# Joining the first stages of a two-layer block into one program section, and loading the expert layers' weights one stage ahead

## The chip, the cores and the metric

The kernel runs on one core of one Trainium2 chip. Its time is the device time of one execution in microseconds (us). The core has a matrix engine (TensorE, in the profile PE, its weight loads PEld), a vector engine (VectorE, DVE), an activation engine (ScalarE, ACT), a general engine (GpSimd, POOL) and a control engine (SyncE, SP) that in this kernel issues nearly all transfers (DMAs). The engines run side by side and wait for each other by semaphores. The work is written as a row of blocks; a block begins when all five engines have left the one before.

## The reference

Two layers are applied to x (64 sequences of 32 tokens, 512 wide). Cut to what matters:

```python
def _L0_cond_ref(u, length, log_dt, C, log_A_real, A_imag, D):
    mask = (jnp.arange(Lq) < length[:, None]).astype(u.dtype)
    u_m = u * mask[:, None, :]
    kernel = _get_kernel(log_dt, C, log_A_real, A_imag, Lq)      # filter taps, 32 filters of 512
    y = irfft(rfft(u_m) * rfft(kernel))[..., :Lq]                # a causal convolution
    return (y + u_m * D[:, None]) * mask[:, None, :]
def _L0_ffn_ref(x, W_base, b_base, W_gate, A, B):                # _L1_ffn_ref has the same form
    result = x @ W_base.T + b_base
    probs = softmax(x @ W_gate.T)                                # 8 experts, the two best are used
    h = einsum('bnd,erd->bner', x, A)
    return result + einsum('bner,eor->bno', h * route_w, B) * SCALING
x = x + _L0_ffn_ref(_L0_cond_ref(x, ...), ...)
x = x + _L1_ffn_ref(_L1_cond_ref(x, ...), ...)                   # paged attention with rotary positions
```

`_get_kernel` sums 64 damped complex exponentials for each filter. The attention layer reads a cache of keys of 64 pages, and turns query and key by angles that depend on the position.

## The kernel before, in words

The blocks run in this order.

1. `s4d_taps`. SP loads the constants, the filter parameters, the lengths, x in reversed order (`um`, 4 tiles of 1 MB) and the first key pages. DVE computes the filter taps in one long chain of small and middle-sized instructions, in which ACT computes sines; POOL masks `um` by the lengths. PE turns (transposes) the cache of keys in 16 pieces (`turn_keys`): 8 pieces, then the 64 small products that make the taps, then the other 8. ACT copies each turned piece out of PSUM, SP stores it and loads the next piece. When all 16 are stored, SP writes the taps to DRAM.
2. `convolve`. For each of 32 filters SP reads the taps back in Toeplitz form (`cv_toe`, 256 KB), PE multiplies, DVE masks the result into `y_t`. POOL computes the rotary angles from the positions, which SP loads after the first 8 Toeplitz tiles (`cv_leni`, read in single elements); ACT computes their sines.
3. `ffn`, first time (tag 0). SP loads the layer's weights (`f_g`, `f_bias`, `f_a`, `f_w`, `f_lb`). PE computes the gate's logits (L585), turns them (L590), and DVE picks the two best experts in a chain of 19 instructions (L516 to L539). For each of four column groups PE computes `h` (L613), the base product (L620, 16 matrix products in 32 records of the profile), turns the routing weights (L598), spreads them (L604), and adds the expert product (L627). POOL computes the rotary tables `ta` and `tb` meanwhile.
4. `project`, `attention`, `output_projection`, which the diff touches only by one call.
5. `ffn`, second time (tag 1), and the end.

In `ffn` the semaphore `s_ev` counts results taken out of the PSUM banks 1 to 4. Before the base product of each bank PE waits for `s_ev`, and DVE gives the first four counts as credits only after the routing chain is done:

```python
                done["route"] = line.n
                credits(e, s_ev, KB)
```

In `s4d_taps` the step size `log_dt` is read straight into the layout in which it is used, in single elements of 4 bytes:

```python
                    src = bass.AP(tensor=dram["L0_cond_log_dt"].tensor, offset=half, ap=[[0, NS], [2, HP]])
```

The order of the work is written out by hand. An engine does its instructions in that order, and a wait holds up all that stands behind it on its engine.

Of the kernel before, what the change touches and what calls it, by code (L numbers as in the profile page):

```python
# [15 lines left out]
F32 = mybir.dt.float32  # L16
# [128 lines left out]
def s4d_taps(nc, ps, dram, taps, cst, um, mrow, k_t):  # L145
# [6 lines left out]

    with ExitStack() as ctx:
        sb = lambda n, s, d=F32: ctx.enter_context(nc.sbuf_tensor("s4_" + n, s, d))
        sem = lambda n: ctx.enter_context(nc.semaphore("s4_" + n))
        TB = 4
        k_in = sb("k_in", [P, TB, HK * D])
        k_out = sb("k_out", [P, TB, PPT, HK, PSIZE])
        s_kt, s_kc = sem("kt"), sem("kc")
        s_ki, s_ko = ([sem(f"{n}{q}") for q in range(TB)] for n in ("ki", "ko"))  # L160
        leni = sb("leni", [P, B], I32)
        lenf = sb("lenf", [P, B])
        mrev = sb("mrev", [P, KB, B])
# [6 lines left out]
        shape = [P, HP, NMUL]  # L170
        arg, mag, t1, t2, t3, ang, sa, ca, sn, cs, er, ei = (
            sb(n, shape) for n in ("arg", "mag", "t1", "t2", "t3", "ang", "sa", "ca", "sn", "cs", "er", "ei"))
# [3 lines left out]
        s_in, s_v, s_sin, s_u, s_k, s_ev, s_out, s_len, s_x, s_g = (  # L176
            sem(n) for n in ("in", "v", "sin", "u", "k", "ev", "out", "len", "x", "g"))
        done = {}
        mul = cst[:, C_MUL:C_MUL + NMUL]
        with nc.Block() as block:  # L180
            @block.sync
            def _(e):
                e.dma_start(cst[:, :], dram["cst"]).then_inc(s_in, 16)
                for half in range(2):
                    src = bass.AP(tensor=dram["L0_cond_log_dt"].tensor, offset=half, ap=[[0, NS], [2, HP]])
                    e.dma_start(raw[half * NS:(half + 1) * NS, 0, :], src, allow_slow_non_contiguous=True).then_inc(s_in, 16)
# [4 lines left out]
                src = bass.AP(tensor=dram["itok_B_8_3872"].tensor, offset=0, ap=[[0, P], [1, B]])  # L191
                e.dma_start(leni[:, :], src).then_inc(s_len, 16)
                for k in range(KB):
                    e.dma_start(um[:, k, :, :], dram["x_rev"][k * P:(k + 1) * P, :, :]).then_inc(s_x, 16)

                for n in range(TB):
                    e.dma_start(k_in[:, n, :], dram["k_cache"][n * P:(n + 1) * P, :]).then_inc(s_ki[n], 16)
                k_rows = k_t.rearrange("(t n d) x -> t d n x", n=PPT, d=P)

                def store(t, q):  # L200
                    e.wait_ge(s_kc, (t + 1) * 2 + 2)
                    t = slice(t, t + 1) if isinstance(t, int) else bass.ds(t, 1)
                    e.dma_start(k_rows[t, :, :, :].rearrange("o d n x -> (o d) n x"),
                                k_out[:, q, :, :, :].rearrange("p n g k -> p n (g k)")).then_inc(s_ko[q], 16)

                with e.Fori(0, KT // TB - 1) as i:
                    for q in range(TB):
                        store(i * TB + q, q)
                        e.dma_start(k_in[:, q, :], dram["k_cache"][bass.ds((i * TB + q + TB) * P, P), :]).then_inc(s_ki[q], 16)
                for q in range(TB):  # L210
                    store(KT - TB + q, q)
                for q in range(TB):
                    e.wait_ge(s_ko[q], 16 * KT // TB)

                e.wait_ge(s_ev, 1)
                e.dma_start(taps[:, P:KPW].rearrange("h (a b) -> a h b", b=32),
                            kev[:, :, :, :].rearrange("a i t b -> a (i t) b")).then_inc(s_out, 16)
                e.dma_start(taps[:, 0:P], zeros[:, :]).then_inc(s_out, 16)
                e.wait_ge(s_out, 32)

            @block.vector
            def _(e):
# [3 lines left out]
                e.wait_ge(s_in, 16 * 7)  # L226
                flat = lambda x: x.rearrange("p a b -> p (a b)")
# [8 lines left out]
                mulb = spread(mul, 1, HP)  # L236
                v(lambda e: e.tensor_tensor(ang[:, :, :], spread(dai, 2, NMUL), mulb, ALU.mult))
                reduce_angle(v, flat(ang[:, :, :]), flat(t1[:, :, :]), flat(sa[:, :, :]), flat(ca[:, :, :]))
                done["angles"] = line.n
                v(lambda e: e.tensor_tensor(arg[:, :, :], spread(dar, 2, NMUL), mulb, ALU.mult))  # L240
                exp_exact(v, flat(arg[:, :, :]), flat(mag[:, :, :]), flat(t1[:, :, :]), flat(t2[:, :, :]), flat(t3[:, :, :]))
# [4 lines left out]
                zr, zi, nr, ni, t, u = w[3], ei[:, :, 1], w[4], w[5], w[6], w[7]  # L246
# [3 lines left out]
                v(lambda e: e.tensor_tensor(t, ci, zi, ALU.mult))  # L250
                v(lambda e: e.tensor_tensor(nr, nr, t, ALU.subtract))
                v(lambda e: e.tensor_tensor(ni, cr, zi, ALU.mult))
                v(lambda e: e.tensor_tensor(t, ci, zr, ALU.mult))
                v(lambda e: e.tensor_tensor(ni, ni, t, ALU.add))
                sr, si, den = w[8], w[9], w[10]
                v(lambda e: e.tensor_tensor(sr, nr, ar, ALU.mult))
                v(lambda e: e.tensor_tensor(t, ni, ai[:, :], ALU.mult))
                v(lambda e: e.tensor_tensor(sr, sr, t, ALU.add))
                v(lambda e: e.tensor_tensor(si, ni, ar, ALU.mult))
                v(lambda e: e.tensor_tensor(t, nr, ai[:, :], ALU.mult))  # L260
                v(lambda e: e.tensor_tensor(si, si, t, ALU.subtract))
                v(lambda e: e.tensor_tensor(den, ar, ar, ALU.mult))
                v(lambda e: e.tensor_tensor(t, ai[:, :], ai[:, :], ALU.mult))
# [1143 lines left out]
```

## Time and profile before

| | |
|---|---|
| time, median of 3 runs | 2720.36 us (2719.50 to 2720.91) |
| the profiled execution's own time | 2722.63 us |
| its span | 2720.6 us |
| busy, share of the span | PE 93%, PEld 79%, DVE 69%, ACT 47%, POOL 30% |
| DMA, mean over the span | 187 GB/s |
| first block begins, second block's first transfer | 0 us, 109.18 us |
| first `ffn`: first product of the gate | 173.55 us |
| second `ffn`: first product of the gate | 2597.58 us |

The time of a run and the span of its trace differ by 2 us, which lie before and after the span. The busy shares are means over stages with quite different limits: over most of the span PE is busy nine tenths of each slice, in the first slices it is not.

### The profile page before, as it was taken

The numbers are of one execution on the slowest core, as the hardware profiler recorded it, in microseconds if no ns is written. First come the engines' busy times: TensorE is split into PE (matmuls) and PEld (weight loads), VectorE is DVE, ScalarE is ACT, GpSimd is POOL, SyncE is SP. The second block draws the span as 40 slices with busy tenths as digits, with TensorE's granted clock in tenths as the row PEclk, the third lists the DMA queues.
The fourth block names the chain that finished last, engine by engine and source line by source line (L and its number), as shares of the span: only waits on it lengthen the run. The fifth ranks groups of instructions, "written<-read, shape, count | busy, mean of one in ns | idle before, by whom it ended". The sixth has DMA issues, their size and how long they took to land. (4 is left out here: it accounts for less than half of the span.)

```text
span 2720.6 us, 53012 instructions
## 1 busy us (share of the span) xinstructions
PE 2540.0 (93%) x15632; PEld 2139.9 (79%) x15632; DVE 1867.8 (69%) x3327; ACT 1282.3 (47%) x3654; POOL 808.8 (30%) x743
## 2 busy tenths in 40 slices
PE   2479899999998899999999999999999979999989
PEld 1453588777776689999999999999999967777733
DVE  5242599999995088888888888888888854444311
ACT  1101355555553256666666666666666641111100
POOL 3070166666663022222222222222222231212000
PEclk9689999999998999999999999999999989999989
DMA  5441133332334478888888888888888844343212
GB/s 193 162 158 62 58 96 109 94 95 93 112 93 138 146 251 272 295 271 290 276 290 273 291 274 292 274 286 279 288 277 286 280 149 124 108 123 108 62 69 79
DMA packets 432385, 508.52 MB, mean 187 GB/s; under 512 B 39860, under 2 KB 352468, under 8 KB 431828
## 3 DMA queue, kind: packets, MB, share of 16 engines
q1 hardware_dynamic: 395476, 373.71, 41.9%
q0 software_dynamic: 36864, 134.23, 15.5%
q8 instruction: 25, 0.41, 0.1%
q14 instruction: 20, 0.16, 0.0%
HBM read 407.07 MB, written 100.75 MB: 187 GB/s over the span
## 5 line engine op out<-in xcount | busy, mean ns | idle before, releaser
L1079 PE MATMUL ps<-at_v_raw,at_pt 128*128 128x128 f32 x4096 | 541.1, 275 | 0.6 <-DMA at_v_raw<-v_cache,at_idx 0.6
L1079 PEld LDWEIGHTS ps<-at_v_raw,at_pt 128*128 128x128 f32 x4096 | 497.7, 192 | 1.0 <-DMA at_v_raw<-v_cache,at_idx 1.0
L1179 ACT ACTIVATE at_pt<-ps 128x512 f32<-128x512 f32 x512 | 305.1, 596 | 339.8 <-PE ps L1063 326.1
L1146 DVE CUSTOM_DVE_ANT_0 at_sm<-ps,at_mask 128x544 f32<-128x544 f32 x512 | 367.9, 719 | 91.3 <-PE ps L1054 45.4
L868 POOL TENSOR_TENSOR pr_m<-pr_qn,tb 128x256 f32<-128x256 f32 x320 | 331.6, 1056 | 311.7 <-DVE pr_qn L837 296.5
L1190 ACT ACTIVATE at_pr<-at_sm,at_nm 128x544 f32<-128x544 f32 x512 | 383.9, 750 | 72.1 <-DVE at_nm L1146 59.5
L1017 POOL DMA_INDIRECT at_v_raw<-v_cache,at_idx x256 | 307.5, 1201 | 113.1 <-issue 62.3
L702 PE MATMUL ps<-pr_hi,xh 128*128 (+1 forms) x768 | 319.8, 416 | 13.1 <-DVE pr_lo L691 8.7
L1139 DVE TENSOR_TENSOR at_k_lo<-shared,at_k_hi 128x1088 fp32r<-128x1088 f32 x256 | 325.5, 1272 | 0.0
L1054 PE MATMUL ps<-at_k_hi,at_q_hi 128*128 128x272 f32 x1024 | 295.9, 370 | 13.5 <-DVE at_k_lo L1139 13.5
L1063 PE MATMUL ps<-constants,at_pr 128*128 128x128 f32 x2048 | 307.9, 273 | 0.0
L703 PE MATMUL ps<-pr_lo,xh 128*128 (+1 forms) x768 | 305.4, 398 | 0.0
L704 PE MATMUL ps<-pr_hi,xl 128*128 (+1 forms) x768 | 304.5, 397 | 0.0
L795 ACT ACTIVATE pr_sq<-ps 128x128 f32<-128x128 f32 x640 | 168.0, 277 | 235.6 <-DVE pr_ss L830 225.1
L1023 POOL COPY at_idx<-at_rows 128x4 uint32 (+1 forms) x64 | 12.1, 189 | 799.5 <-PE ps L1086 795.6
L1063 PEld LDWEIGHTS ps<-constants,at_pr 128*128 128x128 f32 x2048 | 245.0, 140 | 0.5 <-issue 0.5
L1292 DVE TENSOR_TENSOR att<-att,ps 128x512 f32<-128x512 f32 x128 | 79.4, 682 | 220.1 <-PE ps L1312 220.1
L1054 PEld LDWEIGHTS ps<-at_k_hi,at_q_hi 128*128 128x128 f32 x1024 | 165.8, 192 | 74.4 <-issue 72.8
L1310 PE MATMUL ps<-op_o_hi,op_w_hi 128*128 128x512 f32 x512 | 205.6, 402 | 16.4 <-POOL op_w_lo L1251 16.4
L1054 PE MATMUL ps<-at_k_hi,at_q_lo 128*128 128x272 f32 x1024 | 214.6, 291 | 0.0
L1054 PE MATMUL ps<-at_k_lo,at_q_hi 128*128 128x272 f32 x1024 | 211.5, 288 | 0.0
L1312 PE MATMUL ps<-op_o_hi,op_w_lo 128*128 128x512 f32 x512 | 205.4, 401 | 0.0
(197 smaller groups left out, 4423.1 us busy)
## 6 DMA issues: line engine op xcount, KB each, us to landing
shared<-k_t SPq DMA_DIRECT2D x1024, 128.0 KB, 4.3
qk_t<-pr_stage SPq DMA_DIRECT2D x160, 256.0 KB, 2.3
shared<-qk_t SPq DMA_DIRECT2D x64, 512.0 KB, 7.7
o_t<-at_ot SPq DMA_DIRECT2D x64, 512.0 KB, 5.9
o_raw<-o_t SPq DMA_DIRECT2D x32, 1024.0 KB, 5.9
w_first<-wqkv SPq DMA_DIRECT2D x12, 1024.0 KB, 5.9
s_k_in<-k_cache SPq DMA_DIRECT2D x16, 512.0 KB, 7.2
k_t<-s_k_out SPq DMA_DIRECT2D x16, 512.0 KB, 6.3
```

The lines of the kernel that those rows point to most:

```text
L702: e.matmul(out, xh[:, k, cols], hi, start=(k == 0), stop=False)
L703: e.matmul(out, xh[:, k, cols], lo, start=False, stop=False)
L704: last = e.matmul(out, xl[:, k, cols], hi, start=False, stop=(k == KB - 1))
L868: ins = e.tensor_tensor(heads(m2[:, q, :])[:, :, a], heads(qn[:, q, :])[:, :, b], table(tb, i, j - 3, a), ALU.mult)
L1017: e.indirect_dma_start(out=v_raw[:, q, c, :], out_offset=None, in_=dram["v_cache"], in_offset=bass.IndirectOffsetOnAxis(ap=idx[:, q, c:c + ...
L1054: last = e.matmul(ps[:, 2 * r + h, 0:W], a[:, q, mine], b[:, w, g % 2, h * W:(h + 1) * W], start=first, stop=end)
L1063: last = e.transpose(ps_w[:, c * P:(c + 1) * P], pr[:, w, k, c * P:(c + 1) * P], ident)
L1079: last = e.matmul(ps[:, 5 + w, k * D:(k + 1) * D], pt[:, r, c * P:(c + 1) * P], v_raw[:, q, c, g * D:(g + 1) * D], start=(k == 0 and c == ...
L1139: e.tensor_tensor(two(k_lo), raw, two(k_hi).bitcast(F32), ALU.subtract).then_inc(s_lo, 1)
L1146: e.tensor_tensor_reduce(out=halves(sm[:, r, :]), in0=ps[:, 2 * r:2 * r + 2, 0:W], in1=halves(mask[:, q, :]), scale=-SC, scalar=3e38, op0= ...
L1179: e.activation(pt[:, r, :], ps_w, ACT.Copy).then_inc(s_pt, 1)
L1190: e.activation(pr[:, w, k, :], sm[:, r, :], ACT.Exp, bias=nm[:, at], scale=-1.0, accum_out=su[:, at]).then_inc(s_e, 1)
```

## The change

The two first blocks become one, `prologue`. In it:

- `log_dt` is read as whole rows to all partitions and picked apart by two DVE copies; so is the list of positions, which DVE picks apart with four copies.
- The constants, the lengths, the positions, `um` and the zeros of the taps are loaded or stored by ACT's queue, beside SP's.
- `um` is no longer masked. The output row was masked before and still is.
- PE turns 9 pieces of keys, makes the taps, and then runs the convolution, with one of the other 7 pieces behind every fourth filter. ACT copies the taps out of PSUM, writes them, and issues the Toeplitz loads, between its copies of the late pieces. There are 6 Toeplitz buffers in place of 8.
- The rotary angles are computed by DVE, between the taps and the first convolution result, in 10 instructions (POOL before, in 13).

In `ffn` the weights are loaded by the block before: at the end of `prologue`'s list on SP, and behind the first group of the output projection. The credits are gone: the base products of the first column group wait for nothing. POOL begins the rotary tables only when the routing chain is done. Some buffers share one room of memory, and `w_first` moves to the other side of it.

```diff
-def s4d_taps(nc, ps, dram, taps, cst, um, mrow, k_t):
+def prologue(nc, ps, dram, taps, cst, um, mrow, k_t, y_t, cos, sin, room, inputs):
...
-                e.dma_start(cst[:, :], dram["cst"]).then_inc(s_in, 16)
-                for half in range(2):
-                    src = bass.AP(tensor=dram["L0_cond_log_dt"].tensor, offset=half, ap=[[0, NS], [2, HP]])
-                    e.dma_start(raw[half * NS:(half + 1) * NS, 0, :], src, allow_slow_non_contiguous=True).then_inc(s_in, 16)
+                src = bass.AP(tensor=dram["L0_cond_log_dt"].tensor, offset=0, ap=[[0, P], [1, S]])
+                e.dma_start(log_dt[:, :], src).then_inc(s_in, 16)
...
+                for n in range(KT):
+                    e.wait_ge(s_kc, 2 * (n + 1))
+                    e.dma_start(k_rows[n:n + 1, :, :, :].rearrange("o d n x -> (o d) n x"),
+                                k_out[:, n % TB, :, :, :].rearrange("p n g k -> p n (g k)")).then_inc(s_ko[n % TB], 16)
+                    if n + TB < KT:
+                        load(n + TB)
+                inputs.load(e, dram, ("w0", "b0", "g0", "a0", "lb0"))
...
-                e.wait_ge(s_x, 16 * KB)
-                for k in range(KB):
-                    e.tensor_tensor(um[:, k, :, :], um[:, k, :, :], spread(mrev[:, k, :], 1, S), ALU.mult)
...
             @block.scalar
+                e.dma_start(cst[:, :], dram["cst"]).then_inc(s_cst, 16)
+                for n, name in enumerate(("itok_B_8_3872", "itok_B_207_1644")):
+                    src = bass.AP(tensor=dram[name].tensor, offset=0, ap=[[0, P], [1, B]])
+                    e.dma_start(leni[:, n, :], src).then_inc(s_len, 16)
+                for k in range(KB):
+                    e.dma_start(um[:, k, :, :], dram["x_rev"][k * P:(k + 1) * P, :, :]).then_inc(s_x, 16)
...
+                e.wait_ge(s_ev, 1)
+                e.dma_start(taps[:, P:KPW].rearrange("h (a b) -> a h b", b=32),
+                            kev[:, :, :, :].rearrange("a i t b -> a (i t) b")).then_inc(s_out, 16)
+                e.wait_ge(s_out, 32)
+                for h in range(TOE):
+                    load(h)
+                e.wait_ge(s_v, done["rope"])
+                for x in (sin, cos):
+                    e.activation(x, x, ACT.Sin).then_inc(s_rope, 1)
+                for h in range(S):
+                    if h + TOE < S:
+                        e.wait_ge(s_mm, h + 1)
+                        load(h + TOE)
+                    if late(h):
+                        lay_out(late(h))
...
             @block.tensor
+                for h in range(S):
+                    e.wait_ge(s_toe[h % TOE], 16 * (h // TOE + 1))
+                    wait(e, s_y, h - YB + 1)
+                    for d in range(KB):
+                        last = e.matmul(ps[:, h % YB, d * B:KB * B], toe[:, h % TOE, d * P:(d + 1) * P],
+                                        um[:, 0:KB - d, h:h + 1, :].rearrange("p k o b -> p k (o b)"),
+                                        start=(d == 0), stop=(d == KB - 1))
+                    last.then_inc(s_mm, 1)
+                    if late(h):
+                        turn(late(h))
@@ ffn @@
-                credits(e, s_ev, KB)
...
+                    e.wait_ge(s_nw, 32)
+                    e.wait_ge(s_v, done["route"])
+                    rope_tables(e, s_tab, tables[0], tables[1], nw, tables[2], tables[3])
...
-                        e.wait_ge(s_ev, i * KB + ob + 1)
+                        wait(e, s_ev, (i - 1) * KB + ob + 1)
@@ output_projection @@
                 turn(0)
+                inputs.load(e, dram, ("w1", "b1", "g1", "a1", "lb1"))
```

On SP the transfers of the first block stood in this order before (`s_raw` takes `log_dt` and `log_a`, `s_ai`, `s_cc` and `s_dvec` the other filter parameters):

```order
L183 DMA constants<-cst 128x897
L186 DMA s_raw<-L_cond_log_dt 64x16x1 x2
L187 DMA s_raw<-log_a 128x16
L188 DMA s_ai<-a_imag 128x16
L189 DMA s_cc<-c 128x32
L190 DMA s_dvec<-L_cond_D 1x32
L192 DMA s_leni<-itok_B_3872 128x64
L194 DMA um<-x_rev 128x2048 x4
L197 DMA s_k_in<-k_cache 128x1024 x4
```

Now the same place on SP reads:

```order
L191 DMA s_log_dt<-L_cond_log_dt 128x32
L192 DMA s_raw<-log_a 128x16
L193 DMA s_ai<-a_imag 128x16
L194 DMA s_cc<-c 128x32
L195 DMA s_dvec<-L_cond_D 1x32
L198 DMA s_k_in<-k_cache 128x1024 x4
```

The constants, the lengths and `um` have left SP's list. They stand on ACT, whose list from the start of the block to the first convolution's refills is:

```order
L301 DMA constants<-cst 128x897
L304 DMA s_leni<-itok_B_3872 128x64
L304 DMA s_leni<-itok_B_1644 128x64
L306 DMA um<-x_rev 128x2048 x4
L308 DMA taps<-s_zeros 32x128 [waits s4_v]
...
L333 ACTIVATE s_kev<-ps 16x16x32 [waits s4_k]
...
L336 DMA taps<-s_kev 16x32x32 [waits s4_ev]
L322 DMA s_toe<-taps 128x512 [waits s4_out]
...
L343 ACTIVATE shared<-shared 128x1024 [waits s4_v]
...
L322 DMA s_toe<-taps 128x512 [waits s4_mm] x4
L316 ACTIVATE s_k_out<-ps 128x4x4x32 [waits s4_kt,s4_ko1]
L316 ACTIVATE s_k_out<-ps 128x4x4x32 [waits s4_kt]
```

Each Toeplitz refill now waits on ACT for PE (`s4_mm`), and four refills stand between two copies of a turned piece (`s4_kt`). On PE the first column group of `ffn` read before:

```order
L613 MATMUL ps<-shared,f_a 128x512 [waits f0_in]
L613 MATMUL ps<-shared,f_a 128x512 x3
L620 MATMUL ps<-shared,f_w 128x512 [waits f0_ev]
L620 MATMUL ps<-shared,f_w 128x512 x3
...
L598 MATMUL ps<-constants,f_route 8x128 [waits f0_v]
```

and reads now:

```order
L592 MATMUL ps<-shared,f_a 128x512 [waits f0_s_in]
L592 MATMUL ps<-shared,f_a 128x512 x3
L599 MATMUL ps<-shared,f_w 128x512 x16
L577 MATMUL ps<-constants,f_route 8x128 [waits f0_v]
```

The four waits for `f0_ev` are gone from the 16 base products; the wait for the routing chain (`f0_v`) stands behind them, at the turning of the routing weights.

## Rows read from the trace of the kernel before

**Rows 1.** Stretches: busy PE, PEld, DVE, ACT, POOL, then PE clock, DMA share, GB/s.

```profile
5.00:10.00 5.00, 0.00 (x0) 0.00 (x0) 0.00 (x0) 0.00 (x0) 0.00 (x0) 1.00 0.05 0
30.00:35.00 5.00, 0.00 (x0) 0.00 (x0) 4.69 (x10) 0.00 (x0) 2.47 (x4) 1.00 1.00 418
77.00:84.00 7.00, 6.44 (x125) 6.44 (x126) 0.47 (x2) 0.00 (x0) 0.00 (x0) 0.50 0.01 2
142.00:150.00 8.00, 8.00 (x54) 7.64 (x54) 4.02 (x7) 0.00 (x0) 7.75 (x4) 0.99 0.70 189
```

**Rows 2.** Instructions in order of time: start, us, engine, line, operation, count.

```profile
1.19 1.45 SPq L186 DMA_DIRECT2D s_raw<-L_cond_log_dt  x2
```

**Rows 3.** The same view, the chain of the taps on DVE with POOL beside it.

```profile
27.11 0.18 DVE L114 TENSOR_SCALAR s_raw<-s_raw 128x32 f32<-128x32 f32 x1 [26.13 <-DMA s_dvec<-L_cond_D]
31.11 0.96 DVE L237 TENSOR_TENSOR s_ang<-s_small,constants 128x768 f32<-128x768 f32 x1
36.87 0.56 DVE L140 TENSOR_SCALAR s_ang<-s_sa 128x768 f32<-128x768 f32 x1
36.97 19.99 POOL L296 TENSOR_TENSOR um<-um,s_mrev 128x2048 f32<-128x2048 f32 x4 [4.21 <-DMA um<-x_rev]
37.46 4.75 DVE L141 TENSOR_SCALAR s_ca<-s_sa 128x768 f32<-128x768 f32 x1
42.24 5.13 DVE L142 TENSOR_TENSOR s_ca<-s_ang,s_ca 128x768 f32<-128x768 f32 x1
47.41 5.18 DVE L240 TENSOR_TENSOR s_arg<-s_small,constants 128x768 f32<-128x768 f32 x1
52.62 4.75 DVE L114 TENSOR_SCALAR s_arg<-s_arg 128x768 f32<-128x768 f32 x1
77.56 0.28 PE L336 MATMUL ps<-s_er,s_ur 64*16 64x32 f32 x2 [11.88 <-DVE s_ui L276]
```

**Rows 4.** The same view, from the taps' products to the end of the convolution.

```profile
84.28 5.31 PE L326 MATMUL ps<-constants,s_k_in 128*128 128x128 f32 x32
92.61 1.09 PE L326 MATMUL ps<-constants,s_k_in 128*128 128x128 f32 x8 [3.02 <-DMA s_k_in<-k_cache]
109.18 3.71 SPq L364 DMA_DIRECT2D cv_toe<-taps  x8
112.64 12.55 PE L396 MATMUL ps<-um,cv_toe 128*128 x64 [10.21 <-DMA cv_toe<-taps]
137.32 31.43 PE L396 MATMUL ps<-um,cv_toe 128*128 x192 [12.12 <-DMA cv_toe<-taps]
```

**Rows 5.** Transfers by line: count, KB each, median us from issue to landing.

```profile
cv_toe<-taps SPq DMA_DIRECT2D x32, 256.0 KB, 3.5
cv_leni<-itok_B SPq DMA_DIRECT2D x4, 2.0 KB, 15.2
taps<-s_kev SPq DMA_DIRECT2D x1, 64.0 KB, 2.4
```

**Rows 6.** The same view, the first `ffn` and what precedes the second.

```profile
173.55 15.24 PE L585 MATMUL ps<-shared,f_g 128*8 128x512 f32 x32 [4.80 <-DMA f_g<-g]
190.55 3.70 PE L613 MATMUL ps<-shared,f_a 128*128 128x512 f32 x8
207.58 15.39 PE L620 MATMUL ps<-shared,f_w 128*128 128x512 f32 x32 [13.33 <-DVEq L101]
2592.20 2.48 DVE L1292 TENSOR_TENSOR att<-att,ps 128x512 f32<-128x512 f32 x4 [8.88 <-PE ps L1312]
```

**Rows 7.** Who waited for whom, PE, from 2560 us to the end.

```profile
PE ps L585 <- DMA f_g<-g: 5.4, 1, 5.4
PE ps L620 <- DVEq L101: 2.6, 1, 2.6
```

**Rows 8.** The chain of waits that ended last, its end: start, us, step.

```profile
2622.29 15.70 PE ps L620 x32
2653.20 13.93 PE ps L620 x32
```

More of the change, by code:

```diff
@@ L196, in _ @@
                 for n in range(TB):
-                    e.dma_start(k_in[:, n, :], dram["k_cache"][n * P:(n + 1) * P, :]).then_inc(s_ki[n], 16)
+                    load(n)
                 k_rows = k_t.rearrange("(t n d) x -> t d n x", n=PPT, d=P)
[L200 to L204, printed above, removed]
@@ L225, in _ @@
                 v(lambda e: e.memset(zeros[:, :], 0.0))
-                e.wait_ge(s_in, 16 * 7)
-                flat = lambda x: x.rearrange("p a b -> p (a b)")
+                done["zeros"] = line.n
+                e.wait_ge(s_in, 16 * 5)
+                for half in range(2):
+                    part = slice(half * NS, (half + 1) * NS)
+                    mine = log_dt[part, :].rearrange("p (i two) -> p two i", two=2)[:, half:half + 1, :].rearrange("p o i -> p (o i)")
+                    v(lambda e, part=part, mine=mine: e.tensor_copy(raw[part, 0, :], mine))
                 w = [small[:, i, :] for i in range(12)]
@@ new lines, in _ @@
+                v(lambda e: e.tensor_scalar(pos[:, :], pos[:, :], cst[:, C_MOD:C_MOD + 1], None, ALU.add))
+                e.wait_ge(s_kv, 2)
+                d = kev[0:1, :, :, 0:1].rearrange("a i t b -> a (i t b)")
+                e.tensor_tensor(d, d, dvec[:, :], ALU.add).then_inc(s_ev, 1)
+                v(lambda e: e.tensor_tensor(f, spread(pos[:, :], 2, H), spread(cst[:, C_FREQ:C_FREQ + H], 1, NT), ALU.mult))
+                reduce_angle(v, flat(f), flat(t), flat(sin), flat(cos))
+                done["rope"] = line.n
@@ L330, in _, with turn @@
-                turn_keys(0, 2)
+                def turn(n):
+                    q = n % TB
+                    e.wait_ge(s_ki[q], 16 * (n // TB + 1))
+                    wait(e, s_kc, 2 * (n - 1))
+                    for half in range(2):
+                        for g in range(HK // 2):
+                            x = slice((half * HK // 2 + g) * D, (half * HK // 2 + g + 1) * D)
+                            last = e.transpose(ps[:, 4 + 2 * (n % 2) + half, g * P:(g + 1) * P], k_in[:, q, x],
+                                               cst[:, C_ID:C_ID + P])
+                        last.then_inc(s_kt, 1)
@@ L331, in _ @@
+                e.wait_ge(s_cst, 16)
+                for n in range(EARLY):
+                    turn(n)
                 e.wait_ge(s_u, 1)
@@ L434, in rope_tables, with __init__, load, ffn @@
     e.tensor_scalar(tb[:, :, 0:H], tb[:, :, 0:H], -1.0, None, ALU.mult)
[L437 to L443 removed]
+class Inputs:
+    def __init__(self, nc, ctx, tag, side=None):
+        sb = lambda n, s: ctx.enter_context(nc.sbuf_tensor(f"f{tag}_{n}", s, F32, side=side))
+        self.w = sb("w", [P, KB, L])
+        self.a = sb("a", [P, KB, E * R])
+        self.g = sb("g", [P, KB, E])
+        self.lb = sb("lb", [E * R, L])
+        self.bias = sb("bias", [P, KB])
+        self.s_g, self.s_in = (ctx.enter_context(nc.semaphore(f"f{tag}_{n}")) for n in ("s_g", "s_in"))
+    def load(self, e, dram, names):
+        w_n, b_n, g_n, a_n, lb_n = names
+        e.dma_start(self.g[:, :, :], dram[g_n].rearrange("(k p) e -> p k e", p=P)).then_inc(self.s_g, 16)
+        e.dma_start(self.bias[:, :], dram[b_n]).then_inc(self.s_in, 16)
+        e.dma_start(self.a[:, :, :], dram[a_n].rearrange("(k p) r -> p k r", p=P)).then_inc(self.s_in, 16)
+        e.dma_start(self.w[:, :, :], dram[w_n].rearrange("(k p) o -> p k o", p=P)).then_inc(self.s_in, 16)
+        e.dma_start(self.lb[:, :], dram[lb_n]).then_inc(self.s_in, 16)
+def ffn(nc, ps, dram, inputs, tag, act, src, out, scaling, cst, halves=None, tables=None, ahead=None):
     NB = T // 512
```

289 lines of the change are left out of this document (102 added, 187 removed).

## The prediction

> **What bounds the kernel now.** I read the slices of the span first: PE is busy nine tenths or more in most of them, so only a stage in which PE waits can give much. Two kinds are touched: everything before the first `ffn`, and the routing chains of both `ffn`s. The stretches of the start show the first cause [rows 1]: from 5 to 10 us nothing moves at all, while from 30 to 35 us the same 16 engines carry 418 GB/s. The issues before that silence [rows 2] are the two transfers of `log_dt`, 2048 elements of 4 bytes; the first DVE instruction waits until 27.11 us for the last small input queued behind them [rows 3]. Then DVE's chain sets the pace to 77.56 us, and four of its instructions take about 5 us each while POOL masks `um`; the same kinds take 0.96 and 0.56 us alone [rows 3]. The taps are made by 84.28 us, but the first Toeplitz load is issued at 109.18 us [rows 4]: eight key pieces, their stores and the end of the block lie between. The convolution itself, 112.64 to 168.75 us, stands still for 12.12 us on a Toeplitz tile [rows 4], queued behind the positions, again single elements (15.2 us to landing for 2 KB [rows 5]). In the first `ffn` the gate starts 4.80 us after the convolution for want of its weights, and the base product waits 13.33 us for the routing chain [rows 6]; in the second the two waits are 5.4 and 2.6 us [rows 7]. All of these lie on the path that sets the end, since each block waits for the one before. I go by the gate's first product, 173.55 us now [rows 6].
>
> **Step 1, inputs.** The five small loads go first on SP without the single elements. An issue takes 3.71 / 8 = 0.46 us [rows 4], 0.7 for a scattered one [rows 2], so all are out at about 3.5 us; to landing the nearest small transfer takes 2.4 us [rows 5], which is 5.9. I take 7.0, since 4 MB of `um` and the constants now flow beside them on another queue. Bounds 5.4 and 12. Saved: 27.11 − 7.0 = 20.1 us. Two copies of the new layout cost at most 0.2 us each: −0.4.
>
> The Trainium skill, page "DMA: Bandwidth & Descriptors", section "Queues, rings and completion order", says that SP's and ACT's queues are rings on the same 16 engines, which take them in turn by whole packets. By that rule a small input issued late waits for whole packets of `um`; it is rival A. No row here has two such queues at once.
>
> **Step 2, the chain on DVE.** Without the mask on POOL the four long instructions return to their twins: (4.75 − 0.56) + (5.13 − 0.96) + (5.18 − 0.96) + (4.75 − 0.56) = 16.8 us [rows 3]. POOL has nothing to do in the new block, so I take all of it. The chain was 77.56 − 27.11 = 50.45 us and becomes 50.45 − 16.8 + 0.4 = 34.1; products start at 41.1. ACT's sines now stand behind two key copies and one more table load: ready at about 22, needed at 32, so hidden. The PE products stand behind 9 turned pieces instead of 8. At 418 GB/s `um` and the first 4 pieces (6 MB) are in by about 18 us; a further piece with its store is 1 MB, 2.6 us at the same rate, so piece 9 comes at 31 to 37 us, hidden by 4 us or more; late by 4 at the worst.
>
> **Step 3, taps to Toeplitz.** The products keep their 84.28 − 77.56 = 6.7 us (clock at the lower level, 0.50 [rows 1]): done at 47.8. What followed took 109.18 − 84.28 = 24.9 us [rows 4]. Now: two small ACT copies, 1.2 us (twice 0.6, bounded by the 0.6 of a DVE result of the same order), one DVE add with its waits 0.5, issue 0.35 and landing 2.4 [rows 5]: 4.4 us. Saved 20.5. The first product follows a load by 112.64 − 109.18 = 3.5 us as before: it starts at 55.7.
>
> **Step 4, the convolution.** Eight filters took 12.55 us, the other 24 took 31.43 [rows 4], each group with a slow start after idleness. That makes (31.43 − 12.55) / 16 = 1.18 us per filter and 3.1 us per start. New: 32 × 1.18 + 3.1 = 40.9. Seven late pieces at 1.09 us each on PE [rows 4] add 7.6: 48.5, against 168.75 − 112.64 = 56.1 now. Saved 7.6. The refills: ACT issues filter h + 6 when h is done, at most 0.45 us each; two key copies (1.7 us with their gap) stand before every fourth. A refill has five filters of lead, over 6 us, for 3.5 us of landing [rows 5], so I take 0. But toes, loads and stores together are 2 MB in every 5.9 us, 340 of the 418 GB/s seen, so landing may stretch: up to +8. DVE's rotary angles (10 instructions of 0.75 to 1.3 us, scaled from 768 to 1024 columns by [rows 3], 10.5 us) start with the taps' store and end 4 us into the convolution; four PSUM banks cover 7.9 us of it: 0. The two sines behind them on ACT (about 1 us each) delay refill 7 to about 6.5 us into it; with landing 10.0, needed at 11.4: 0, at worst +2. The convolution ends at 104.2 us.
>
> **Step 5, into the first `ffn`.** The gap of 4.8 us [rows 6] becomes the last DVE result, 0.6 us, and the change of block, 1.3 us in all by my estimate: its weights are issued behind the last key store, some 3 us before the end. Saved 3.5; if that store is late, 0 to 3 less. Gate at 105.5. Sum so far: 20.1 − 0.4 + 16.8 + 20.5 + 7.6 + 3.5 = 68.1, and 173.6 − 68.1 is that 105.5.
>
> **Step 6, the first `ffn`.** The base product follows `h` at once: 13.3 us of waiting goes, and its slow start, 15.39 − 13.93 = 1.5 [rows 6, 8]. The gate took 15.24 us with a slow start of the same kind; with 1.3 us of idleness before it I take 1.0 back (0 to 1.5). The wait for the spread routing weights stays as it is, behind the base product. The routing chain gets rid of POOL beside it, but that is worth nothing on the path: slow as it was it took 3.7 + 13.3 = 17.0 us [rows 6] and now lies beside 3.7 + 13.9 = 17.6 us of products. Sum 15.8. POOL's rotary tables move to the time from routing on. There DVE takes sums out of PSUM; in the convolution DVE's results with one operand in PSUM took 4.02 / 7 = 0.57 us while POOL was busy 7.75 of 8 us [rows 1], so they are not held up. The low halves (two SBUF operands) can be, to about 2 us each in the first group; each base product gives DVE 13.9 us for little else: 0.
>
> **Step 7, the second `ffn`.** Of 5.4 us before the gate the last accumulation on DVE, 2.48 us [rows 6], and the change of block stay: 2.6 saved. The base product's wait 2.6 [rows 7] and slow start 15.70 − 13.93 = 1.8 [rows 8] go, and I add 0.5 for a shorter slow start elsewhere (0 to 3): 7.5. The five loads behind the first group of the output projection cost 5 × 0.46 us of SP and 1.5 MB (3.7 us at 418 GB/s); the tile next in line is issued about one unit of products ahead, and such a unit leaves DVE 8.88 us of idleness [rows 6], so 0, at worst 1.
>
> **Sum.** 68.1 + 15.8 + 7.5 = 91.4 us. The profiled execution would take 2722.6 − 91.4 = 2631.2 (span 2629.2, and 2.0 around it); it lies 2.3 above the median of the runs, so for the median 2720.4 − 91.4 = 2629.0. The unknown costs are one-sided, so I take 2630.
>
> **Rivals.**
> A. The small inputs wait behind `um`. `um`'s rows are 8 KB; eight rows on one engine are 64 KB, 2.5 us at 418 / 16 = 26 GB/s [rows 1]. Two of the five loads are issued after the flow of `um` begins: +5, at most +8 with the constants: 2636. For it: nothing orders the two queues. Against: the first three are out before.
> B. The refills of the convolution run dry behind ACT's key copies. +1.1 us for each of 7 pieces, or +8: 2638. For it: 340 GB/s. Against: lead of over 6 us against 3.5.
> C. The clock warms up where I left it low, since PE turns keys shortly before the taps and idles less: products half as long (−3.3), convolution start −2, expert products −2: 2622.
> D. Slower. ACT's single list turns the convolution into a round trip: if every refill came only after the filter before was done, one filter would cost 1.2 + 0.45 + 3.5 us and a share of the key copies (0.4), 5.6 us in place of 1.5. That is +129 us for 32, and 2759. It decides once a filter costs 1.5 + 91 / 32 = 4.4 us. For it: refills do wait on PE in one list with the key copies. Against: six buffers; only a missing overlap of all of them does it.
> E. The waits removed only uncover the next: PE's base product would wait as long for `f_w`, landing late. Price: most of 13.3 us, 2642. Against: it is issued before the block ends, 1 MB needs 2.5 us at 418 GB/s beside 2.4 of landing, and the gate's 15 us of products come first.
>
> **How the numbers follow.** Forecast 0.62; A 0.14; B 0.10; C 0.08; E 0.03; D 0.03. The range reaches to C and its bounds below (2614), to A and B together above (2630 + 8 + 8, and some for the block's end, 2650); outside remain D and some of C, under 2 in 10. A measurement of this kernel tells about 0.2%, 5 us, from no change; only D is slower, so faster 0.95, same 0.02, slower 0.03.
>
> **What would show it.** Right: the first DVE instruction after its inputs at 6 to 8 us; no DVE instruction of 768 columns over 1 us in the chain; taps' products at about 41; Toeplitz loads at about 52; a convolution of about 49 us with no wait over 2 us on a Toeplitz tile; the gate at 104 to 108; no wait between `h` and the base product in either `ffn`, and the wait for the expert product still there. Wrong: the gate after 115, long waits of PE on Toeplitz tiles or of DVE on its inputs, or a base product that still starts 13 us after `h`.

## Result, and the profile after

| | kernel before | kernel after |
|---|---|---|
| median of 4 runs | 2720.64 us (2719.50 to 2721.84) | 2625.51 us (2624.20 to 2627.74) |
| ratio after / before | | 0.9651, 95% interval 0.9634 to 0.9668 |
| span of the profiled execution | 2720.6 us | 2622.4 us |

The forecast was 2630.0 us, with a range of 2614 to 2650: the time lies inside it, 4.5 us below the forecast. The gain between the two profiled executions, 98.2 us of span, is 3 us larger than that of the medians, 95.1: the one before took 2722.63 us, 2.0 above its median, and the one after is the fastest of its four (2624.2 us), 1.3 below.

Two marks are read off every trace below: the first product of the first gate and of the second. With the first product of the block that follows the first `ffn` they cut the span in four.

| us of the profiled execution | before | after | gained | forecast |
|---|---|---|---|---|
| start to first gate | 173.55 | 103.36 | 70.2 | 68.1 |
| first gate to `project` | 134.0 | 116.1 | 17.9 | 15.8 |
| `project` to second gate | 2290.0 | 2286.6 | 3.4 | 2.6 |
| second gate to the end | 123.0 | 116.3 | 6.7 | 4.9 |

Stretches of the kernel after (busy PE, PEld, DVE, ACT, POOL, PE clock, DMA share, GB/s); they answer to [rows 1]:

```profile
4.00:6.00 2.00, 0.00 (x0) 0.00 (x0) 0.00 (x0) 0.00 (x0) 0.00 (x0) 1.00 0.47 136
10.00:15.00 5.00, 1.48 (x7) 1.51 (x8) 4.51 (x15) 0.36 (x1) 0.00 (x0) 1.00 1.02 426
63.00:99.00 36.00, 36.00 (x258) 34.69 (x257) 15.27 (x26) 7.59 (x14) 0.00 (x0) 1.00 0.92 310
```

The silence of 5 to 10 us is gone: 136 GB/s at 4 to 6 us and all 16 engines busy from 10 us on. In the convolution (third row) PE does not stand still at all, and the transfers run at 310 GB/s.

DVE's chain and the first products of the kernel after (start us, us, engine, line, operation, in brackets the idle time before and what ended it); they answer to [rows 3]:

```profile
8.29 0.37 DVE L223 COPY s_raw<-s_log_dt 64x16 f32<-64x16 f32 x2 [7.31 <-DMA s_dvec<-L_cond_D]
18.78 0.56 DVE L141 TENSOR_SCALAR s_cs<-s_sn 128x768 f32<-128x768 f32 x1
19.37 0.96 DVE L142 TENSOR_TENSOR s_cs<-s_ang,s_cs 128x768 f32<-128x768 f32 x1
20.36 0.96 DVE L237 TENSOR_TENSOR s_ang<-s_small,constants 128x768 f32<-128x768 f32 x1
21.36 0.56 DVE L114 TENSOR_SCALAR s_ang<-s_ang 128x768 f32<-128x768 f32 x1
35.98 1.97 PE L360 MATMUL ps<-constants,s_k_in 128*128 128x128 f32 x8 [0.67 <-DMA s_k_in<-k_cache]
42.11 0.28 PE L372 MATMUL ps<-s_er,s_ur 64*16 64x32 f32 x2 [4.15 <-DVE s_ui L273]
```

DVE starts 18.8 us earlier, and the four instructions that took 4.75 to 5.18 us take 0.56 and 0.96 (the last four DVE rows). PE has turned its ninth key piece (L360) by 37.95 us and then waits 4.15 us for the chain.

From the taps to the convolution in the kernel after (same columns); they answer to [rows 4]:

```profile
50.33 0.33 ACTq L336 DMA_DIRECT2D taps<-s_kev  x1
52.55 2.76 ACTq L322 DMA_DIRECT2D s_toe<-taps  x6
55.89 7.03 PE L380 MATMUL ps<-um,s_toe 128*128 128x256 f32 x32 [6.99 <-DMA s_toe<-taps]
62.76 1.04 PE L360 MATMUL ps<-constants,s_k_in 128*128 128x128 f32 x8
63.64 4.92 PE L380 MATMUL ps<-um,s_toe 128*128 128x256 f32 x32
97.48 4.92 PE L380 MATMUL ps<-um,s_toe 128*128 128x256 f32 x32
```

A key piece (L360) stands behind every fourth filter, and the next filters follow it without a wait.

The first `ffn` of the kernel after; it answers to [rows 6]:

```profile
103.36 13.89 PE L564 MATMUL ps<-shared,f_g 128*8 128x512 f32 x32 [0.95 <-PEq L187]
119.00 3.70 PE L592 MATMUL ps<-shared,f_a 128*128 128x512 f32 x8
122.54 13.90 PE L599 MATMUL ps<-shared,f_w 128*128 128x512 f32 x32
136.27 0.60 PE L577 MATMUL ps<-constants,f_route 128*8 128x128 f32 x4
140.25 3.70 PE L606 MATMUL ps<-f_room,f_lb 128*128 128x512 f32 x8 [1.58 <-DVE f_room L518]
```

The gate waits 0.95 us for the change of block instead of 4.80 for weights, and the base product (L599) follows `h` (L592) without a gap, where it waited 13.33 us.

The chain of waits of the kernel after in the second `ffn` (start us, us, what); it answers to [rows 8]:

```profile
2506.10 15.61 PE ps L564 x32
2523.52 3.63 PE ps L592 x8
2527.15 13.73 PE ps L599 x32
2544.70 5.40 PE ps L606 x8
```

### The profile page after: what moved, and what is told of

It reads as the page before. It is cut to its first block and busy times, and to the rows that moved or that the text cites. A ratio compares the mean times of both kernels' runs of the same rounds, so it can differ in the third digit from the quotient of the medians.

```text
span 2622.4 us, 52668 instructions
## 1 busy us (share of the span) xinstructions
PE 2524.1 (96%) x15632; PEld 2131.3 (81%) x15632; DVE 1853.3 (71%) x3347; ACT 1285.0 (49%) x3657; POOL 754.8 (29%) x715
## 3 DMA queue, kind: packets, MB, share of 16 engines
q0 software_dynamic: 36864, 134.23, 16.4%
## 5 line engine op out<-in xcount | busy, mean ns | idle before, releaser
L1290 PE MATMUL ps<-op_o_hi,op_w_hi 128*128 128x512 f32 x512 | 205.6, 402 | 15.8 <-POOL op_w_lo L1231 15.8
## 6 DMA issues: line engine op xcount, KB each, us to landing
shared<-k_t SPq DMA_DIRECT2D x1024, 128.0 KB
```

## Experiments

All start from the kernel after. Each row gives the median of four runs, its difference from the kernel after (2625.51 us), and the ratio to runs of the kernel before on the same chip. Those runs had medians of 2722.1 to 2723.3 us in the experiments against 2720.64 beside the kernel after, so the same difference by the ratios, (ratio − 0.9651) × 2720.64, stands beside: between the two columns lies what these runs cannot tell.

| | median us | − after | by ratios | ratio, 95% interval | first gate | to `project` | second gate to end |
|---|---|---|---|---|---|---|---|
| after | 2625.51 | | | 0.9651 (0.9634 to 0.9668) | 103.4 | 116.1 | 116.3 |
| e1_credits | 2631.99 | +6.5 | +3.8 | 0.9665 (0.9649 to 0.9681) | 104.3 | 122.3 | 117.3 |
| e2_tables_early | 2628.14 | +2.6 | −2.2 | 0.9643 (0.9624 to 0.9662) | 104.9 | 119.2 | 115.7 |
| e3_both_back | 2644.50 | +19.0 | +16.3 | 0.9711 (0.9695 to 0.9727) | 104.3 | 132.6 | 119.0 |
| e9_turn_inside_base | 2616.43 | −9.1 | −11.4 | 0.9609 (0.9593 to 0.9625) | 104.5 | 113.7 | 110.4 |
| e4_weights_inside | 2631.64 | +6.1 | +4.9 | 0.9669 (0.9653 to 0.9685) | 105.9 | 117.5 | 117.4 |
| e5_mask_on_pool | 2645.26 | +19.8 | +15.8 | 0.9709 (0.9693 to 0.9726) | 121.1 | 119.0 | 115.9 |
| e6_scattered | 2650.93 | +25.4 | +23.1 | 0.9736 (0.9720 to 0.9753) | 128.0 | 117.8 | 115.8 |
| e8_all_keys_first | 2634.20 | +8.7 | +6.3 | 0.9674 (0.9658 to 0.9690) | 112.8 | 117.8 | 115.8 |
| e7_um_after_inputs | 2626.16 | +0.7 | −2.4 | 0.9642 (0.9626 to 0.9659) | 104.3 | 119.2 | 115.8 |
| e10_both_better | 2616.41 | −9.1 | −10.3 | 0.9613 (0.9597 to 0.9629) | 104.2 | 113.7 | 110.5 |
| e11_two_toes | 2678.50 | +53.0 | +50.9 | 0.9838 (0.9821 to 0.9854) | 154.4 | 120.4 | 116.3 |
| e12_inputs_alone | 2613.87 | −11.6 | −12.8 | 0.9604 (0.9588 to 0.9620) | 102.2 | 113.7 | 110.5 |

The last three columns are of one profiled execution each.

**e1_credits: base products behind the routing chain again.**

```diff
                 done["route"] = line.n
+                credits(e, s_ev, KB)
-                        wait(e, s_ev, (i - 1) * KB + ob + 1)
+                        e.wait_ge(s_ev, i * KB + ob + 1)
```

(and the two later waits on the same semaphore one group further on)

> The changed kernel with the base products of the first column group made to wait for the routing chain again, in both expert layers; the rotary tables still start behind that chain. Theory (the two edits of the layer share one gain): the chain now takes about 6 us beside 3.6 us of products, so PE waits only some 2.5 us, plus a slow start of 1.5 to 1.8 us, in each layer, and in the first the expert product may lose its full clock again (+1.7): +8 to +10 us in all. Rival (the removed wait is worth by itself what it was before, 13.3 + 1.5 and 2.6 + 1.8): +19 us.

```profile
126.28 15.70 PE L600 MATMUL ps<-shared,f_w 128*128 128x512 f32 x32 [2.58 <-DVEq L101]
145.69 5.40 PE L607 MATMUL ps<-f_room,f_lb 128*128 128x512 f32 x8 [1.48 <-DVE f_room L519]
```

The base product waits 2.58 us, as expected, and takes 1.8 us more after it; so it does in the second `ffn` (2.60 us, and 15.70 against 13.90). The cost of 3.8 to 6.5 us lies below the 8 to 10 of the first theory, since in this execution the second gate (13.89 us against 15.6) and the second expert product (3.70 against 5.40) were faster than in the profile of the kernel after, by 3.4 us in parts that the edit leaves as they are. It lies far from the rival's +19: most of the old wait is hidden as long as the tables stay late.

**e2_tables_early: POOL's rotary tables beside the routing chain again.**

```diff
-                    e.wait_ge(s_v, done["route"])
                     rope_tables
```

> The changed kernel with POOL's rotary tables no longer held back until the routing chain is done. Theory: POOL stretches the chain on DVE from 6 to about 17 us again, but PE has 3.6 + 13.9 = 17.5 us of products to do before it needs the result: 0 to +1 us. Rival (the later start of the tables is worth what it takes off the chain): +11 us.

```profile
136.80 0.29 DVE L512 TENSOR_TENSOR f_route<-f_one 128x128 f32<-128x128 f32 x1
124.08 13.90 PE L598 MATMUL ps<-shared,f_w 128*128 128x512 f32 x32
141.79 6.74 PE L605 MATMUL ps<-f_room,f_lb 128*128 128x512 f32 x8 [1.58 <-DVE f_room L518]
```

The routing chain now ends at 137.1 us instead of 125.2 (L512 at 124.89 in the kernel after), 32.2 us after the gate's first product instead of 21.8, and the base product starts at once all the same. The expert product's 6.74 us against 3.70 is all that differs on PE in this layer, and it is not this edit's: e7_um_after_inputs, with the same `ffn` as the kernel after, has 6.77 there. No difference, as expected.

**e3_both_back: both edits undone.**

> Both at once: the base products wait for the routing chain, and the tables run beside it. Theory: now the whole stall is back, 13.3 us and its slow starts in the first layer (about +15 to +17) and 2.6 + 1.8 in the second (+4.4): +19 to +21 us, far more than the sum of the two single steps (8 to 11). Rival (each edit has its own share): the sum of the two single results.

```profile
136.52 15.82 PE L599 MATMUL ps<-shared,f_w 128*128 128x512 f32 x32 [12.84 <-DVEq L101]
```

The 13 us are back (12.84 against 13.33 in [rows 6]). From this kernel on, all on one chip, freeing the base products alone wins 16.4 us (2644.50 to e2's 2628.14) and moving the tables alone 12.5 (to e1's 2631.99). The two are not a sum: either edit by itself hides most of the wait, so undone singly they seem to cost 2.6 and 6.5, and together 19.0 (by the ratios nothing, 3.8 and 16.3).

**e9_turn_inside_base: turning and spreading the first group's routing weights between the base products instead of behind them.**

```diff
                         wait(e, s_ev, (i - 1) * KB + ob + 1)
+                        if i == 0 and ob == 2:
+                            turn_weights(i)
+                        if i == 0 and ob == 3:
+                            expand(i)
-                    if i == 0:
-                        turn_weights(i)
-                        expand(i)
```

> The changed kernel with the routing weights of the first column group turned before the third bank of the base product and spread before the fourth, in both layers, instead of behind all four. Theory: the wait of PE between base product and expert product (3.8 us, of which 1.5 us are the turning and spreading themselves) goes: -2.3 us in each layer, and in the second layer the expert product keeps its clock (5.40 against 3.43 us, -2.0): about -6.5 us. Rival (the wait stays, ended by ACT or DVE): 0.

```profile
130.52 0.60 PE L577 MATMUL ps<-constants,f_route 128*8 128x128 f32 x4
134.49 1.12 PE L583 MATMUL ps<-f_room,constants 8*128 8x512 f32 x2
139.07 3.60 PE L607 MATMUL ps<-f_room,f_lb 128*128 128x512 f32 x8
```

The last wait of the group is gone (the kernel after waits 0.68 and 1.58 us there), and the expert product takes 3.60 us. The gain of 9.1 us exceeds the 6.5 expected. In the second `ffn` 116.3 us became 110.4: some 2.4 of waits, 5.40 − 3.60 = 1.8 in the expert product, and 1.7 in a place that the edit does not touch, the gate:

```profile
2503.56 13.89 PE L564 MATMUL ps<-att,f_g 128*8 128x512 f32 x32 [2.84 <-PEq L1197]
```

In the kernel after it takes 15.6 us behind the same wait of 2.84 us. There the kernel after is the exception: of the twelve kernels with this wait only it and e11 show 15.6 us, the other ten 13.89. A fairer measure of the step is e10 against e7, whose `ffn` is that of the kernel after, both on one chip: 2626.16 − 2616.41 = 9.8 us, of which their profiles show 119.2 − 113.7 = 5.5 in the first layer and 115.8 − 110.5 = 5.3 in the second.

**e4_weights_inside: the expert layers' weights loaded inside `ffn` again.**

```diff
-                inputs.load(e, dram, ("w0", "b0", "g0", "a0", "lb0"))
-                inputs.load(e, dram, ("w1", "b1", "g1", "a1", "lb1"))
+                inputs.load(e, dram, tuple(n + tag for n in ("w", "b", "g", "a", "lb")))
                 if tables:
```

> The changed kernel with both expert layers' weights loaded at the start of the layer itself, as before. Theory: the gate waits for its weights again, 4.8 against 1.0 us in the first layer and 5.4 against 2.8 in the second, and both gates start at the lower clock (15.24 against 13.89, 16.67 against 15.61): +8.8 us. Rival (these loads were hidden beside the end of the block anyway): 0.

```profile
105.87 15.25 PE L564 MATMUL ps<-shared,f_g 128*8 128x512 f32 x32 [2.92 <-DMA f_g<-g]
```

The first gate waits 2.92 us, not the 4.80 of before, and takes 15.25 us instead of 13.89: 3.3 us in the first layer. The second gate waits 4.76 us against 2.84, where the expectation had 5.4. So the measured 4.9 to 6.1 us stay below the 8.8 expected, which took both waits from the kernel before.

**e5_mask_on_pool: the mask of `um` on POOL again.** The kernel after does not mask `um` at all; the edit puts the four products with the mask back, on POOL:

```diff
+            @block.gpsimd
...
+                    e.tensor_tensor(um[:, k, :, :], um[:, k, :, :], spread(mrev[:, k, :], 1, S), ALU.mult).then_inc(s_um, 1)
```

> The changed kernel with the mask of um done by POOL again, four instructions of 5 us from about 19 us on (the output row is masked as well, so the result is the same). Theory: each of the four POOL instructions holds up one DVE instruction with two SBUF operands or with one at double rate, at 4.2 us apiece: taps' products 16.8 us later, +17 us. Rival (DVE's long instructions had another cause, the transfers of um landing at the same time): 0, and no DVE instruction of 768 columns over 1 us.

```profile
22.49 19.73 POOL L312 TENSOR_TENSOR um<-um,s_mrev 128x2048 f32<-128x2048 f32 x4 [12.27 <-DMA um<-x_rev]
22.70 4.77 DVE L116 TENSOR_SCALAR s_t<-s_t 128x768 f32<-128x768 f32 x1
27.50 5.16 DVE L117 SCALAR_TENSOR_TENSOR s_ang<-s_t,s_ang 128x768 f32<-128x768 f32 x1
32.70 5.17 DVE L118 SCALAR_TENSOR_TENSOR s_ang<-s_t,s_ang 128x768 f32<-128x768 f32 x1
37.90 4.74 DVE L119 TENSOR_SCALAR s_t<-s_ang 128x768 f32<-128x768 f32 x1
```

Four POOL instructions, four long DVE instructions, end beside end: the taps' products start 16.9 us later, the 16.8 of step 2. They are four other instructions than in [rows 3]; what counts is which stand beside POOL. The gate stands 17.7 us later; most of what the 19.8 us hold beyond that is the first expert product, 6.64 us in this execution against 3.70. The Trainium skill, page "SBUF — State Buffer", section "Who interferes with whom", says that when a DVE instruction with two SBUF inputs or in a 2-port mode meets a GpSimd one that needs the same pair of ports, the one that comes second fully blocks until the first is done; the steps of 4.7 to 5.2 us agree, POOL's four taking 19.73 / 4 = 4.93.

**e6_scattered: `log_dt` in single elements again.**

```diff
-                src = bass.AP(tensor=dram["L0_cond_log_dt"].tensor, offset=0, ap=[[0, P], [1, S]])
+                for half in range(2):
+                    src = bass.AP(tensor=dram["L0_cond_log_dt"].tensor, offset=half, ap=[[0, NS], [2, HP]])
```

> The changed kernel with log_dt read as 2048 elements of 4 bytes again, on SP, while the constants and um go by ACT's queue. Both theories expect DVE's first instruction at about 24 to 27 us and +16 to +19 us. Theory 1 (the elements occupy the transfer engines themselves): from 5 to 15 us hardly anything moves on either queue, under 50 GB/s. Theory 2 (only SP's own queue stands behind them): um moves meanwhile, at over 200 GB/s from 5 to 15 us.

Three stretches (columns as above):

```profile
4.00:6.00 2.00, 0.00 (x0) 0.00 (x0) 0.00 (x0) 0.00 (x0) 0.00 (x0) 1.00 0.05 1
10.00:15.00 5.00, 0.00 (x0) 0.00 (x0) 0.00 (x0) 0.00 (x0) 0.00 (x0) 1.00 0.08 9
20.00:25.00 5.00, 0.00 (x0) 0.00 (x0) 0.00 (x0) 1.28 (x1) 0.00 (x0) 1.00 0.91 366
```

From 4 to about 15 us next to nothing moves on either queue, although ACT issues the loads of `um` from 2.24 us on; issuing the four took 15.84 us, against 3.22 in the kernel after. Then the 16 engines carry 259 to 366 GB/s, and DVE starts at 33.8 us, later than the 27.11 of before, where no second queue ran. That the small inputs behind the elements then had to share with `um` is my reading; no run separates it. The first theory's mechanism holds, its price (+16 to +19) was 4 to 6 too low.

**e8_all_keys_first: all 16 key pieces ahead of the taps' products.**

```diff
-TB, YB, EARLY, H = 4, 4, 9, D // 2
+TB, YB, EARLY, H = 4, 4, 16, D // 2
```

> The changed kernel with all 16 pieces of keys turned before the taps' products, none during the convolution. Theory: the pieces come at the pace of their transfers, 2.6 us each, so the sixteenth is done at about 56 us and the products start 14 us later, while the convolution gets 7 pieces of 0.9 us shorter: +8 us. Rival (the order of the pieces is worth nothing, PE does the same work): within 1 us.

The taps' products started at 56.10 us instead of 42.11, as worked out, and the convolution at 71.17 instead of 55.89. Free of the seven late pieces it gave back 5.9 of those 15.3 us: the gate stood 9.4 later. Seven pieces inside the convolution cost less than half of what they cost before the products.

**e7_um_after_inputs: ACT issues `um` only when the small inputs have landed.**

```diff
+                e.wait_ge(s_in, 16 * 5)
                 for k in range(KB):
                     e.dma_start(um[:, k, :, :]
```

> The changed kernel with ACT's loads of um held back until the five small inputs have landed. Theory (the small inputs, landed at 8.3 us, wait behind packets of um on the same transfer engines): they land at 5.5 to 6 us, DVE starts 2.3 to 2.8 us earlier, and the whole kernel ends that much earlier, since um is not needed before 50 us: -2.5 us. Rival (the landing time is the small transfers' own): DVE's start unchanged, 0.

Stretch of this kernel:

```profile
4.00:6.00 2.00, 0.00 (x0) 0.00 (x0) 0.00 (x0) 0.00 (x0) 0.00 (x0) 1.00 0.42 111
```

A miss: DVE starts at 8.14 us, not 2.5 earlier. The 16 engines still carry 111 GB/s at 4 to 6 us and 251 at 6 to 8: the key pieces, which SP issues behind the inputs from 2.99 us on, are under way.

**e10_both_better: e9 and e7 together.**

> The changed kernel with both steps: um held back until the small inputs have landed, and the routing weights turned and spread inside the base product. Theory: the gains add up, since they lie in different stages: about -9 us against the changed kernel, 2616 us. Rival: one of them is swallowed by a wait behind it, -6.5 or less.

Its 2616.41 us equal e9's 2616.43, and the first products of the taps start at 42.16 us as before: holding back `um` alone is worth nothing while the key pieces flow.

**e11_two_toes: two Toeplitz buffers instead of six.**

```diff
-    TOE = 6
+    TOE = 2
```

> The changed kernel with two Toeplitz buffers in place of six, the mechanism of the slower case in the prediction in part. Theory: the refills' round trip now bounds the convolution, two filters in 1.2 + 0.45 + 4.8 us (landing as measured in the changed kernel), 3.2 us per filter against 1.2 and the pieces partly inside: about +55 us, PE waiting on Toeplitz tiles nearly every filter. Rival (PE or DVE bounds it all the same): under +10 us.

Waits of PE in this kernel (total us, count, longest):

```profile
PE ps L380 <- DMA s_toe<-taps: 34.9, 19, 6.9
```

As expected, rival D's mechanism exists, and begins when the overlap goes: from its first product to the gate the convolution takes 98.3 us against 47.5. One of the 19 waits, 6.9 us, lies before the first product, as in the kernel after. So of these 50.8 us 34.9 − 6.9 = 28.0 are waits; the other 22.8 are products and key pieces that run longer between them, at a mean granted clock of 0.74. The hit (+53 for +55) is partly luck: a tile landed in 3.2 us here, not the 4.8 taken, and the slower products, left out, made up for it. With six buffers PE waits for a Toeplitz tile once, before the first.

**e12_inputs_alone: e10, and SP's first four key pieces also wait for the small inputs.**

```diff
+                e.wait_ge(s_in, 16 * 5)
                 for n in range(TB):
                     load(n)
```

> The kernel with both steps of before (um held back, routing weights turned inside the base product), and SP's first four key pieces held back too until the small inputs have landed; beside them only the constants and two small lists are under way. Theory: what keeps the small inputs until about 8.2 us is their own handling and the constants, not the key pieces either: DVE starts at 7.5 to 8.3 us, the first key piece comes some 2 us later, which the taps' chain hides: within 1 us of the kernel with both steps (2616.4 us). Rival (the key pieces took the room that um left): DVE starts at 6 us or earlier and the time falls by 2 us.

```profile
6.25 0.37 DVE L224 COPY s_raw<-s_log_dt 64x16 f32<-64x16 f32 x2 [5.28 <-DMA s_dvec<-L_cond_D]
37.68 1.97 PE L362 MATMUL ps<-constants,s_k_in 128*128 128x128 f32 x8 [0.68 <-DMA s_k_in<-k_cache]
40.10 0.28 PE L374 MATMUL ps<-s_er,s_ur 64*16 64x32 f32 x2 [0.45 <-DVE s_ui L274]
```

The first theory falls, its rival holds: with only the constants and two small lists beside them the inputs are there 2.1 us earlier than in e10 (8.35), and all 2.1 arrive at the taps' products (42.16 us in e10) and at the end. So the key pieces alone were enough to delay them. Whether `um` alone would be, no run shows: it was never let flow without the key pieces, and e7's null did not clear it. With 2613.87 us, ratio 0.9604 (0.9588 to 0.9620), this version beats both kernels. Its next bound is in the second row: the ninth key piece ends only 0.45 us before the products.

## Why the prediction was right, step by step

- **Step 1**, start at 7.0, bounds 5.4 to 12: 8.29. The single elements were the cause (e6). The 1.3 us over the forecast are not shown to be rival A's: with `um` held back DVE starts at 8.14 (e7), and only with the key pieces held back too at 6.25 (e12). A cost that I had put at nothing, the inputs' own queue going on with key pieces, is enough for 2 us; rival A's 5 to 8 did not come. The rule quoted from the Trainium skill, page "DMA: Bandwidth & Descriptors", section "Queues, rings and completion order", that the two queues are served in turn on the same engines, is therefore not tested by this start; e6, where elements on SP's queue hold up ACT's loads, agrees that the engines are shared.
- **Step 2**, a chain of 34.1 us: 42.11 − 8.29 = 33.8. Confirmed by e5, 16.9 against 16.8. Piece nine was hidden, with 42.11 − 37.95 = 4.2 us of cover where I had 4 or more. Of rival C nothing came here: the taps' products kept their pace (42.11 to 48.90 us, 6.8 us). The granted clock cannot be read from the trace of the kernel after in this stretch: its column says 1.00, and says 0.50 in e7 beside the same products at the same pace (6.7 us).
- **Step 3**, loads at 52.2 and first product at 55.7: 52.55 and 55.89. From the end of the taps' products to the first Toeplitz load are 52.55 − 48.90 = 3.7 us now, 24.9 before. This is the largest single saving, and no run puts the boundary between the two blocks back: it is read from the two traces alone, and so are the 56.1 − 46.5 = 9.6 us of the convolution.
- **Step 4**, a convolution of 48.5 us: 102.40 − 55.89 = 46.5, without any wait inside. A filter costs (68.40 − 63.64) / 4 = 1.19 us against 1.18. Too high were the slow start (62.76 − 55.89 − 4.76 = 2.1 against 3.1) and the late pieces (63.64 − 62.76 = 0.88 against 1.09, seven times). Rival B stayed away though the landing of a tile rose from the 3.5 us taken to 4.8: six buffers cover it (e11 shows what two do).
- **Step 5**, a gap of 1.3: 0.95. The preloading is worth (2.92 − 0.95) + (15.25 − 13.89) = 3.3 us at this gate by e4's profile, and 4.76 − 2.84 = 1.9 at the second, or 3.6 where the gate takes 13.89 us behind the shorter wait (15.53 in e4).
- **Step 6**, 15.8: measured 17.9. Wait 13.33; base product 15.39 − 13.90 = 1.5 as forecast; gate 15.24 − 13.89 = 1.35, where I took 1.0 and bounded by 1.5; expert product 5.40 − 3.70 = 1.7, which I had at nothing and given to rival C. That term varies from run to run: with the same code and the same 4 us before it, in which PE does only 1.7 us of work, the expert product took 3.70, 5.40 (e8) and 6.77 us (e7). In e7's profile the whole stretch gained 134.0 − 119.2 = 14.8 us, not 17.9, so here the profiled execution of the kernel after was lucky.
- **Step 7**, 7.5: 3.4 before the second gate and 6.7 behind. Of the latter 2.60 is the wait, 1.8 the slow base product (15.70 to 13.90), and the rest the gate and the expert product, both less slow. Here are the second gate of the kernel before, and its expert product:

```profile
2597.58 16.65 PE L585 MATMUL ps<-att,f_g 128*8 128x512 f32 x32 [5.42 <-DMA f_g<-g]
2641.69 6.58 PE L627 MATMUL ps<-f_hw,f_lb 128*128 128x512 f32 x8 [1.47 <-DVE f_hw L546]
```

  (16.65 − 15.61) + (6.58 − 5.40) = 2.2 us, where I allowed 0.5 for a shorter slow start.

The low halves of the first group, which I let grow to 2 us each behind POOL's tables, came out at 1.3:

```profile
125.33 2.34 POOL L396 TENSOR_TENSOR ta<-shared,f_nw 128x1024 f32<-128x1024 f32 x1 [124.90 <-DVE f_route L512]
144.66 5.27 DVE L530 TENSOR_TENSOR xl<-f_resid,xh 128x512 fp32r<-128x512 f32 x4
```

No wait of PE follows from them, so they cost nothing, as forecast.

In the profile the gain stands 98.2 − 91.4 = 6.8 us above the sum: 2.1 up to the first gate, where the convolution gave 2.0 more than forecast, 2.1 in step 6 and 2.6 in step 7. Of the last two 0.35 + 1.7 + (2.2 − 0.5) = 3.8 us are one kind of term, the time that the same products take after a wait, which I had too small. That part of rival C came in this execution, though its chance was put at 0.08. Rivals D and E are excluded: no wait for a refill, none for `f_w`.

The granted clock tells the three times of the expert product apart. Stretches of exactly that product (columns as above) in the kernel after, in e8 and in e7:

```profile
140.25:143.95 3.70, 3.70 (x10) 1.66 (x11) 2.25 (x3) 1.29 (x3) 3.61 (x3) 1.00 0.00 0
149.68:155.08 5.40, 5.40 (x10) 2.26 (x11) 2.25 (x3) 1.29 (x3) 5.31 (x3) 0.68 0.00 0
141.21:147.98 6.77, 6.77 (x10) 2.79 (x11) 2.25 (x3) 1.72 (x3) 6.68 (x3) 0.54 0.00 0
```

The second gate is the same case: over its first 5 us the mean granted clock was 0.66 in the kernel after (15.6 us) and 1.00 in e7 (13.89 us). As far as the profiles show, the engine did the same before it in each. Not settled is what makes the clock fall in one execution and not in another; no experiment set it, e9 only took the gap away.

## What to carry to other kernels

When a wait of PE goes, price with it the products behind it: after gaps of a few us they ran up to 3.1 us longer here (6.77 against 3.70), and such terms were over half of what the forecast lacked in the profiled execution. Read them from more than one execution. Two edits that shield the same product from the same late result are not a sum: undo each alone and both together before one of them is called useless. And a null from holding one transfer back (e7) clears it only when nothing else takes the room it left.

## What the hardware showed that was not expected

- With 2048 single elements of 4 bytes under way, two transfers on one queue, all 16 engines moved 1 to 11 GB/s from 4 to 14 us (e6), and issuing four loads of 1 MB on the other queue took 15.84 us instead of 3.22.
- Small transfers issued first on their queue landed 2.1 us later when tiles of 0.5 MB followed closely on the same queue (8.35 us in e10, 6.25 in e12).
- The same product with the same gap before it took 3.70, 5.40 or 6.77 us from one execution to the next, at a mean granted clock of 1.00, 0.68 or 0.54, and the second gate 13.89 or 15.6 us behind the same wait of 2.84.
